# Packed output projections and score jobs of four heads in a chain of four attention blocks

## The reference

```
L0: x = softmax_over_queries(q k^T / 8, masked) v @ W_O^T + b_O + x        # 16 heads of 64, keys from ctx
L1: x = layernorm(x + gate * routed(ctx))                                   # gates
L2: x = normalise(x + relu(attn(x, ctx) @ Wo + bo))                         # 16 heads of 16, relu on q, k, v, CAUSAL
L3: x = layernorm(x + mha(x, x, window of 64, slopes) @ swo + sbo)          # 16 heads of 16, BANDED
    x = layernorm(x + mha(x, ctx) @ cwo + cbo)                              # 16 heads of 16, FULL
    x = layernorm(x + gelu(x @ w1 + b1) @ w2 + b2)                          # 1024 hidden
```

## Time and profile before

| | us |
|---|---|
| three runs | 1758.82, 1765.01, 1767.97 (median 1765.01) |
| the profiled execution | 1767.88 |
| its span | 1766.1 |
| TensorE busy | 1555.6 (88%) |
| VectorE busy | 902.9 (51%) |
| ScalarE busy | 739.4 (42%) |
| GpSimd busy | 251.0 (14%) |
| mean granted TensorE clock | 0.936 of full |

### The profile page before, as it was taken

The page is one execution under the profiler, slowest core; times in us unless marked ns, Lnnn a source line. Parts: engine busy times, 40 slices in busy tenths (PEclk is TensorE's granted clock), DMA queues, the critical chain, the costliest instruction groups (busy, mean ns, idle before and its releaser), DMA issues.

```text
span 1766.1 us, 26713 instructions
## 1 busy us (share of the span) xinstructions
PE 1555.6 (88%) x9276; PEld 815.9 (46%) x9308; DVE 902.9 (51%) x2236; ACT 739.4 (42%) x1289; POOL 251.0 (14%) x116
## 2 busy tenths in 40 slices
PE   5999898888999988878999998887899998889786
PEld 2337455434434645632533554563253355465234
DVE  2662665482465365557156437455625635645661
ACT  0761344264265243517236325252724631624352
POOL 1003111201101112110110201211011031112102
PEclk9998898989999889889999979998999997989899
DMA  9002104503100211250310030224111003031300
GB/s 336 1 7 36 37 1 73 108 1 114 50 1 7 36 37 24 50 108 1 113 50 1 7 58 15 50 60 72 43 72 49 1 14 65 2 68 43 59 25 12
DMA packets 44867, 84.13 MB, mean 48 GB/s; under 512 B 10416, under 2 KB 28592, under 8 KB 44464
## 3 DMA queue, kind: packets, MB, share of 16 engines
q1 hardware_dynamic: 39680, 68.98, 15.4%
q10 hardware_dynamic: 5040, 13.28, 3.7%
HBM read 42.37 MB, written 2.10 MB: 25 GB/s over the span
## 4 chain that ended last, share of the span: by engine, by line
PE 61%; issue 15%; DVE 11%; ACT 5%; DMA 3%; ACTq 2%; POOL 2%; DVEq 0%; POOLq 0%
PE ring L1135 7%; PE obank L1145 7%; PE ring L1125 7%; DVE nmax L955 6%; PE ring L1086 5%; PE ring L1378 4%; PE obank L1340 4%; PE ring L1321 3%; PE ring L1201 3%; PE ring L1304 3%; PE ring L1290 3%; PE ring L1107 2%; ACT region_e L709 2%; PE ring L1073 2%; DMA q_all<-q_parts 2%
## 5 line engine op out<-in xcount | busy, mean ns | idle before, releaser
L955 DVE TENSOR_REDUCE nmax<-ring 128x2 f32<-128x1024 f32 (+4 forms) x384 | 318.6, 855 | 175.7 <-PE ring L1290 120.9
L709 ACT ACTIVATE region_e<-ring 128x1024 f32<-128x1024 f32 (+4 forms) x384 | 269.8, 733 | 115.6 <-PE ring L1290 81.2
L819 DVE CUSTOM_DVE_ANT_0 region_d<-ring,maskb 128x512 f32<-128x512 f32 x256 | 165.8, 686 | 101.1 <-issue 101.1
L606 ACT ACTIVATE region_e<-region_d,nmin 128x512 f32<-128x512 f32 x256 | 182.6, 714 | 81.7 <-DVE nmin L819 80.1
L701 ACT ACTIVATE q_all<-ring 2x1024 fp32r<-2x1024 bf16 x96 | 97.6, 1016 | 230.1 <-DVE nmax L955 116.3
L1290 PE MATMUL ring<-cbf 64*128 64x128 bf16 (+1 forms) x2048 | 169.7, 251 | 0.0
L1304 PE MATMUL ring<-k_tiles_a,q_all 64*128 64x512 f32 (+4 forms) x384 | 98.3, 514 | 47.8 <-DMA q_all<-q_parts 40.7
L1135 PE MATMUL ring<-region_q 64*128 64x512 f32 x512 | 126.1, 613 | 5.4 <-ACT region_q L595 5.4
L539 POOL TENSOR_TENSOR nat_x<-nat_n,rows 128x1024 f32<-128x1024 f32 x16 | 37.7, 2354 | 649.9 <-DVE nat_n L864 486.4
L1145 PE MATMUL obank<-region_e,vs 128*64 128x512 f32 x512 | 124.0, 605 | 0.0
L1321 PE MATMUL ring<-q_all,k_tiles_a 64*128 64x512 f32 (+4 forms) x384 | 91.9, 470 | 22.9 <-ACT q_all L701 12.4
(11 more groups left out here) (171 smaller groups left out, 2226.3 us busy)
## 6 DMA issues: line engine op xcount, KB each, us to landing
k_tiles_a<-k_parts SPq DMA_DIRECT2D x144, 64.0 KB, 2.3
k_tiles_b<-k_parts SPq DMA_DIRECT2D x144, 64.0 KB, 2.3
q_all<-q_parts ACTq DMA_DIRECT2D x144, 64.0 KB, 3.4
q_all<-q_parts SPq DMA_DIRECT2D x144, 64.0 KB, 3.2
region_b<-in_w_f SPq DMA_DIRECT2D x8, 1024.0 KB, 5.1
wvo<-in_wv SPq DMA_DIRECT2D x4, 1024.0 KB, 8.2
wqk<-in_wq SPq DMA_DIRECT2D x4, 1024.0 KB, 10.1
wqk<-in_wk SPq DMA_DIRECT2D x4, 1024.0 KB, 12.1
```

The source lines that it names most:

```text
L606: ins = act.activation(e0[:, n % E0, h, :], sm0[:, n % 2, h, :], ACT.Exp, bias=nmin0[:, n, h:h + 1], scale=-1.0, accum_out=sum0[:, n, h:h ...
L709: act.activation(e16[:, n % 4, 2 * u:2 * u + 2, 0:nq], slot((a, "B", g, kt, u))[:, :, 0:nq], ACT.Exp)\
L819: ins = dve.tensor_tensor_reduce(out=sm0[:, n % 2, h, :], in0=slot(("S0", p, kt))[:, h, :], in1=maskb[:, :], scale=-1.0, scalar=3.0e38, op ...
L955: dve.tensor_reduce(nmax[:, qt, 2 * u:2 * u + 2], slot(name)[:, :, 0:nk], AX.X, ALU.max, negate=True)\
```

## The change

- `wide(a, kind, i)` is true for all BANDED jobs, for CAUSAL pass A on query tiles 0 and 1, and for CAUSAL pass B on key tiles 2 and 3. Such a job does all four heads of the group: the two planes u lie side by side in each bank (2 x 192 or 2 x 256 columns). It has four score matmuls, and four mask matmuls that cover both planes by a broadcast table; one reduction or one exponential drains it. FULL keeps jobs of two heads. The job list of a group goes from 17 to 9 jobs (BANDED) and to 13 (CAUSAL).
- The projection weights are packed: two groups share 128 rows (`packed`), 16 rows per head and group, so `out_heads` runs over two packs instead of four groups. `head_out` multiplies in the transposed layout, where sums need no second transpose, into `o_pack`; after every second group one transpose writes `oT[:, g // 2, :]`. It waits for the odd group of a pack.
- The bias is no longer in the weights. GpSimd adds `sbo` to the banded residual, `cbo` goes into the row `b1n` once at the start, and for CAUSAL it prepares `degen * mean_o + bo2` in `nat_y` in two passes, which VectorE adds in one operation per half.
- The ones for the softmax sums are one column per head instead of 16.

The diff, cut to these parts (renames of the tile `wide` to `spread` and semaphore counts are left out):

```diff
+def wide(a, kind, i):
+
+    if a == CAUSAL:
+        return i < NT // 2 if kind == "A" else i >= NT // 2
+    return a == BANDED
+
+
+def pieces(a, kind, i):
+
+    return (0,) if wide(a, kind, i) else (0, 1)
+
+
+def ahead(a, g, n):
+
+    i, u = divmod(n, 2)
+    return [("A", g, i, u)] if g < GROUPS and u in pieces(a, "A", i) else []
...
     for i in range(2 * NT):
-        steps.append(("B", g) + divmod(i, 2))
+        kt, u = divmod(i, 2)
+        if u in pieces(a, "B", kt):
+            steps.append(("B", g, kt, u))
         if i < NT:
-            steps += ahead(g + 1, NT + i)
-            if i < 2 and g:
-                steps.append(("V", g - 1, 2 + i))
+            steps += ahead(a, g + 1, NT + i)
+            if g and i in ((0, 2) if a == BANDED else (0, 1)):
+                steps.append(("V", g - 1, 3 if i else 2))
...
-                    one = ones[:, 0:NT * H].rearrange("p (t h) -> p t h", t=NT).unsqueeze(3).broadcast_to([P, NT, H, DH])
-                    pool.tensor_tensor(v[:, :, :, DH:2 * DH], one, one, ALU.mult).then_inc(ones_ready, 1)
+                    one = ones[:, 0:NT * H].rearrange("p (t h) -> p t h", t=NT)
+                    pool.tensor_tensor(v[:, :, :, DH], one, one, ALU.mult).then_inc(ones_ready, 1)
...
                 residual(0, "ga1", "be1")
+                for name in (("cnt",), ("meanO",)):
+                    pool.wait_ge(*drained_by(name, b))
+                link(pool.tensor_tensor(nat_y[:, :, :], mean_o[:, :].unsqueeze(1).broadcast_to([P, NT, D]),
+                                        degen[:, :].unsqueeze(2).broadcast_to([P, NT, D]), ALU.mult))
+                pool.tensor_tensor(nat_y[:, :, :], nat_y[:, :, :], wide_row("bo2"), ALU.add).then_inc(base_ready, 1)
...
+                pool.wait_ge(norm_ready, b * 5 + 2)
+                pool.tensor_tensor(nat_x[:, :, :], nat_n[:, :, :], wide_row("sbo"), ALU.add).then_inc(resid_ready, 1)
...
+                    if wide(a, "B", kt):
+                        act.activation(e16[:, n % 4, :, 0:nq].rearrange("p (u i) q -> p i u q", u=2),
+                                       slot((a, "B", g, kt, u))[:, :, 0:2 * nq].rearrange("p i (u q) -> p i u q", u=2), ACT.Exp)\
+                            .then_inc(*ends_drain((a, "B", g, kt, u)))
+                        return
...
+                    if wide(a, "A", qt):
+                        dve.tensor_reduce(nmax[:, qt, :].rearrange("p (u i) -> p i u", u=2),
+                                          slot(name)[:, :, 0:2 * nk].rearrange("p i (u k) -> p i u k", u=2), AX.X, ALU.max, negate=True)\
+                            .then_inc(*ends_drain(name))
+                        return
...
-                    sums = rbuf[:, :].rearrange("p (c r) -> p c r", r=32)[:, :, DH]
+                    turned = rbuf[:, :].rearrange("p (c r) -> p c r", r=32)
+                    sums = turned[:, :, DH]
                     if a == CAUSAL:
                         link(dve.tensor_scalar(rsum[:, :], sums, 1e-30, None, ALU.max))
                         sums = rsum[:, :]
                     link(dve.reciprocal(rsum[:, :], sums))
-                    link(dve.transpose(rbuf[:, :].rearrange("p (c r) -> p c r", r=32),
-                                       rsum[:, :].unsqueeze(2).broadcast_to([P, S // 32, 32])))
-                    dve.tensor_tensor(oT[:, g, :], o, rbuf[:, :], ALU.mult).then_inc(out_drained, 1)
+                    half = DH * (g % 2)
+                    ins = dve.tensor_tensor(o_pack[:, :].rearrange("p (c r) -> p c r", r=32)[:, :, half:half + DH], turned[:, :, 0:DH],
+                                            rsum[:, :].unsqueeze(2).broadcast_to([P, S // 32, DH]), ALU.mult)
+                    if g % 2:
+                        link(ins)
+                        ins = dve.transpose(oT[:, g // 2, :], o_pack[:, :])
+                    ins.then_inc(out_drained, 1)
...
-                    for i in range(2):
-                        t = 2 * j + i
-                        ins = dve.scalar_tensor_tensor(out=nat_y[:, t, :], in0=mean_o[:, :], scalar=degen[:, t:t + 1],
-                                                       in1=slot(("O2", j))[:, i, 0:D], op0=ALU.mult, op1=ALU.add)
-                    ins.then_inc(*ends_drain(("O2", j)))
+                    part = slice(2 * j, 2 * j + 2)
+                    dve.tensor_tensor(nat_y[:, part, :], slot(("O2", j))[:, :, 0:D], nat_y[:, part, :], ALU.add)\
+                        .then_inc(*ends_drain(("O2", j)))
...
-                drain_out("OS", nat_n)
+                dve.wait_ge(resid_ready, b * 5 + 2)
+                drain_out("OS", nat_x)
...
-                def mask_heads(dst, table, n, whole, lo, at):
+                def mask_heads(dst, n, table, part, cols):
 
                     for half in range(2):
                         for i in range(2):
                             own = slice(64 * i, 64 * i + 64)
-                            ins = pe.matmul(dst[:, i, lo:lo + n], cb("halves", P, own, at=half * P), cb(table, n, own, at=half * whole + at),
-                                            start=False, stop=(half == 1))
+                            mask = cb(table, cols.stop - cols.start, own, at=half * part + cols.start).unsqueeze(1).broadcast_to(
+                                [64, n, cols.stop - cols.start])
+                            ins = pe.matmul(dst(i), cb("halves", P, own, at=half * P), mask, start=False, stop=(half == 1),
+                                            skip_group_check=(n == 2))
+                    return ins
...
+                def scores(dst, stationary, moving, n, us, a):
+
+                    for at, u in enumerate(us):
+                        for i in range(2):
+                            own = slice(64 * i, 64 * i + 64)
+                            ins = pe.matmul(dst[:, i, at * n:(at + 1) * n], stationary(own, u), moving(own, u),
+                                            start=(at == 0), stop=(a == FULL), skip_group_check=(len(us) == 2))
...
+                    us = (0, 1) if wide(a, "A", qt) else (u,)
+                    ins = scores(dst, lambda own, v: q_tiles[g][own, v, qt * P:(qt + 1) * P],
+                                 lambda own, v: k_tiles[g][own, v, k0:k0 + nk], nk, us, a)
+                    by_head = dst[:, :, 0:len(us) * nk].rearrange("p i (u k) -> p i u k", u=len(us))
                     if a == BANDED:
-                        ins = mask_heads(dst, "bandA", nk, BAND, 0, BAND - nk)
+                        ins = mask_heads(lambda i: by_head[:, i, :, :], len(us), "bandA", BAND, slice(BAND - nk, BAND))
                     elif a == CAUSAL:
-                        ins = mask_heads(dst, "maskA", P, P, nk - P, 0)
+                        ins = mask_heads(lambda i: by_head[:, i, :, nk - P:nk], len(us), "maskA", P, slice(0, P))
...
-                    for t in range(GROUPS):
-                        pe.wait_ge(out_drained, b * OUT_ITER + PAIRS + a * GROUPS + t + 1)
+                    for t in range(PACKS):
+                        pe.wait_ge(out_drained, b * OUT_ITER + PAIRS + a * GROUPS + 2 * t + 2)
                         for j in range(2):
                             for i in range(2):
                                 m = 2 * j + i
                                 ins = pe.matmul(dst[j][:, i, 0:D], oT[:, t, m * P:(m + 1) * P], w_out[a][:, t, :],
-                                                start=(t == 0), stop=(t == GROUPS - 1))
-                            if t == GROUPS - 1:
+                                                start=(t == 0), stop=(t == PACKS - 1))
+                            if t == PACKS - 1:
...
-def padded(w, bias, a):
+def packed(w):
 
     import numpy as np
-    out = np.zeros((GROUPS, 4, 32, D), np.float32)
+    out = np.zeros((PACKS, 4, 2, DH, D), np.float32)
     for g in range(GROUPS):
         for s, h in enumerate(heads_of(g)):
-            out[g, s, 0:DH] = w[h * DH:(h + 1) * DH]
-    out[0, 0, DH] = bias
-    return out.reshape(GROUPS * P, D)
+            out[g // 2, s, g % 2] = w[h * DH:(h + 1) * DH]
+    return out.reshape(PACKS * P, D)
```

More of the change, by code:

```diff
@@ L37 @@
 GROUPS = H // 4
+PACKS = GROUPS // 2
 FF = 1024
@@ L115, in attention_jobs @@
 def attention_jobs(a):
-    jobs = [(a, "A", 0, qt, u) for qt in range(NT) for u in range(2)]
+    jobs = [(a, "A", 0, qt, u) for qt in range(NT) for u in pieces(a, "A", qt)]
     for g in range(GROUPS):
-        jobs += [(a,) + step for step in group_steps(g) if step[0] in "ABT"]
+        jobs += [(a,) + step for step in group_steps(a, g) if step[0] in "ABT"]
     return jobs
@@ L261, in build @@
         u_b = region_q[:, 1024 + D:1024 + 2 * D]
-        wide = sb("wide", [P, DT, P])
+        spread = sb("spread", [P, DT, P])
         km = sb("km", [P, NT])
@@ L675, in _ @@
                 act.wait_ge(*filled_by(("vpT",), b))
-                act.activation(wide[:, :, :], slot(("vpT",))[:, 0, 0:D].rearrange("p (t n) -> p t n", t=DT), ACT.Copy)\
```

(31 more changed lines are left out.)

72 lines of the change are left out of this document (34 added, 38 removed).

## The result

| | before | after |
|---|---|---|
| median of the runs beside each other, us | 1765.95 (4 runs) | 1707.12 (4 runs, 1701.98 to 1713.66) |
| ratio, 95% interval | | 0.9676 [0.9627, 0.9725] |
| profiled execution, its span | 1767.88, 1766.1 | 1713.66, 1711.9 |
| TensorE busy | 1555.6 | 1495.4 |
| mean granted clock | 0.936 | 0.930 |

What follows compares the result with a forecast made beforehand. The prediction took TensorE as the bound, busy 88% of the span and 61% of the chain. Gains of 34.6 + 1.6 + 18.4 + 12.4 + 1.4 = 68.4 us from 1767.9 gave 1699.5, predicted as 1697, range 1670 to 1732.

Steps and rivals of the forecast that it cites:

- The packed projections: Output projections: 16 records instead of 32; gains per batch 3.45 us behind banded, 2.7 full, 2.5 causal; 34.6 in all.
- the head output walk: Last head output before the second pack: transpose, reciprocal, 256-element multiply, transpose and gaps, 2.24 us in all.
- The wide job every 0.55: Banded attention: one wide 192-column job every 0.55 us (bounds 0.49 and 0.62), against 0.60 to 0.62 for two narrow jobs.
- the clock rival: Banded and causal loops and tails fall to the 1.2 GHz level, a wide job costs 1.05 us: 1815 us; chance 0.07.
- the place where row and rule differed: Banded score jobs: the rule on weight-load overlap put a wide job above 0.8 us; the profile row gave 0.55, which was kept.
- Costs at nothing: GpSimd's three more passes of 2.35 us per batch, smaller ones columns and halved weight loads were taken as hidden, costing nothing.
- The rival of the shared port: GpSimd presets hold up the head output's multiply in 6 of 12 places per batch, 29 us: 1725 us; chance 0.05.
- causal loops: Steady causal attention groups with half the jobs wide: 0.9 us gained per loop (0.6 to 1.1), twice per batch.
- the two banded loops: Steady banded attention groups with wide jobs: 1.7 us gained per loop (1.45 to 1.9), for two loops per batch.
- the packed part: Everything but the wide jobs: projections 34.6 us, head outputs 1.6 and causal residual 1.4 over four batches.
- Only the projections pay: Wide jobs double the ring's grain and eat the banded and causal gains, 30.8 us fall away: 1727 us; chance 0.17.
- More comes: Half-clock stretches shorten or vanish, and the banded and causal loops reach 7.6 and 10.4 us: 1676 us; chance 0.15.

Runs made afterwards that it cites:

- experiment 1: The changed kernel with GpSimd's two new passes issued behind the first query preset of the banded stage: median 1694.49 us, ratio 0.9593 to the kernel before.
- experiment 11: The changed kernel itself, timed once more on the same chip as 12: median 1704.32 us, ratio 0.9669 to the kernel before.
- 12: The kernel of experiment 1, timed once more on another chip: median 1697.81 us, ratio 0.9591 to the kernel before.
- 8: The changed kernel with all score jobs narrow and the two GpSimd passes where the change puts them: median 1735.68 us, ratio 0.9814 to the kernel before.
- experiment 5: The kernel of experiment 1 with all score jobs narrow: median 1723.21 us, ratio 0.9766 to the kernel before.
- 3: The kernel before with the two GpSimd passes added at the place of the change, their result unused: median 1778.25 us, ratio 1.0061 to the kernel before.

## Why the prediction was right, and where it was off

**Held.** The sign, the size within the range, and the main terms. The packed projections: 16 records in 3.45 behind the banded attention, nothing waiting. In the full one the half arrives 18.84 behind the last casts, where before it was 21.62 (850.05 less 828.43): 2.8 gained, 2.7 forecast; the head output walk (2.24) came to 821.79 - 819.58 = 2.21. The wait ahead of the second eight records, forecast at some 0.6, is 0.41 there and 0.62 behind the causal attention. The causal projection gave 2.6 for 2.5, the causal residual 0.36 for 0.35. The multiply of 256 elements: 0.43 for 0.42. The full groups went from 14.59 and 13.71 to 14.57 and 13.28: 0.45 for 0.4. The wide job every 0.55 was 0.51 to 0.54; at the 1.2 GHz level (timeline at 281.41 and 282.45) it was 1.04, where the clock rival had 1.05. Since both nearly double, no run here separates loads from columns as the pace, as I had done. The job of 0.54:

```profile
708.88 0.47 PE L1340 MATMUL ring<-k_tiles_b,q_all 64*128 64x192 f32 x4 [0.47 <-ACT q_all L727]
...
709.39 0.50 PE L1340 MATMUL ring<-q_all,k_tiles_a 64*128 64x192 f32 x4
...
709.93 0.50 PE L1340 MATMUL ring<-k_tiles_b,q_all 64*128 64x192 f32 x4
```

That decides the place where row and rule differed. The weight loads of the middle job, in the same stretch:

```profile
709.36 0.35 PEld L1340 LDWEIGHTS ring<-q_all,k_tiles_a 64*128 64x128 f32 x4
709.73 0.11 PEld L1331 LDWEIGHTS ring<-cbf 64*128 64x128 bf16 x4
```

Loads fill 0.46 of a job's 0.54, and its score matmuls alone have records of 0.50 (their ends are modelled), so most of its columns stream beside loads into the same two row groups. The rule of the Trainium skill, "TensorE: Matmul & The Clock Gate", section "Part 3: Packing small matmuls — row/col tiling", that I had weighed would not allow that; the measurement decides. The same section of the Trainium skill also lets a load that goes to the background weight buffer run ahead; whether these loads do, no run here shows.

**The step that failed** is "Costs at nothing": "Two run right after the first residual, and the presets queued behind them wait for score jobs some 12 us later ... If that cover fails, 2.35 each." I asked who waits for GpSimd's results and queue, not which VectorE operation runs on SBUF beside it. Nobody waited for the passes; the cast and the subtraction waited for GpSimd, and T behind them. The two operations alone are 3.0 longer per batch in the trace of the result. From the first causal cast to the second, four batches together, the traces with the stall are longer by 14.6 (result against experiment 1), 10.0 (11 against 12), 11.8 (8 against 5) and 12.2 (3 against the kernel before); the medians of the same pairs differ by 12.6, 6.5, 12.5 and 10.9. Without the stall the kernel takes 1694.5 and 1697.8 in its two sets of runs, where I had forecast 1697. Part of that closeness is luck: terms that were too high and too low cancel, as the mis-sized terms below show.

**The rival of the shared port** (0.05, 1725) had the mechanism and the wrong place: presets against the head output's multiply. The multiply takes at most 427 ns in all 48 groups, so that never collided. Its victims are not found by the longest VectorE operation but by the one that TensorE waits for.

**Mis-sized terms**, per batch: causal loops 2.8 (11.49 and 11.63 to 10.15 and 10.17) instead of 1.8; causal tail 0.8 instead of 1.1; banded tail 0.7 instead of 1.2; the two banded loops 3.55 instead of 3.4. The kernels without wide jobs show that 0.1 of three of these four loops comes from the shorter head outputs (9.73 to 9.63, 11.63 to 11.49), which I had put down for the full attention alone. In all, the wide jobs measured 28.7 for 30.8 (31 at equal clock), and the packed part, without the stall, 42 (1765.0 to 1723.2) for 37.6.

**"Only the projections pay"** is refuted by experiment 5 against 1. **"The clock falls"** did not come: every steady loop of the profile above ran at 1.00, and in experiment 11 one of sixteen was lower (0.97, a banded loop of 8.05). **"More comes"** did not come either: the causal loops did better than its 10.4, but the banded ones stayed at 7.95 for its 7.6, and the half-clock stretches of the openings stayed.

## What to carry to other kernels

Before work is moved to GpSimd, list which operations of VectorE run in that time: one on 16 elements waited here until the whole GpSimd pass was over (2.41 for 0.23), and if TensorE waits for that operation the idle engine's work is on the path. The trace of before had a warning: the mask operation L780, 512 elements with one SBUF input, takes 0.43 in the first batch and 0.84 to 1.06 in the other three, where it runs beside GpSimd's passes. The mending is cheap: the same passes, started at 630.52 in experiment 1, 17 us after GpSimd fell free, lengthened no operation of VectorE. And read from the trace which engine bounds a stretch before a fall of the clock there is counted as a loss.

## What the runs showed of the hardware

- A 16-element cast with a single SBUF input is held too, and even by a memset (0.76, 1.05 at most, instead of 0.20).
- The last full group has two lengths across the kernels, often within one trace: 13.3 and 14.6 (with the old head outputs 13.7 and 14.7 to 14.9). The windows show the clock in its middle three microseconds, the same work both times: first the changed kernel, then experiment 1.

```profile
796.89:799.89 3.00, 2.77 (x20) 0.98 (x24) 2.58 (x4) 2.01 (x3) 0.00 (x0) 1.00 0.00 0
```

```profile
790.23:793.23 3.00, 2.82 (x12) 0.73 (x12) 2.49 (x3) 1.64 (x2) 0.00 (x0) 0.54 0.00 0
```

TensorE gets through 12 matmul records instead of 20 there, and the group ends 1.3 later. What sets off such a fall in one batch and not in the next, with the same instructions ahead of it, stays open.

- The same in the banded tail, where TensorE is busy most of the time: experiment 5 from the last banded cast to the third head output, in the first and in the second batch.

```profile
300.83:313.15 12.32, 10.78 (x135) 6.21 (x132) 3.94 (x11) 6.90 (x14) 2.97 (x2) 0.72 0.01 2
724.35:733.99 9.64, 8.04 (x135) 4.87 (x132) 3.98 (x13) 6.62 (x14) 3.01 (x2) 1.00 0.01 3
```

The same 135 matmul records take 2.7 longer. So a fall of the clock cost 1.3 and 2.7 in these two stretches, and nothing in the 10.40 group, where VectorE is busy 9.84.
